# Local-attention layers: the feed-forward's inner rows as one plain float32 tensor, and its second product with unsplit float32 weights

## What is computed

```python
def _layer(x, wqkv, qs, ksc, wo, lg, lb, w1, b1, w2, b2):
    h = shift_token(x)
    ...                                  # q, k, v, norm, rotary, local attention
    x = x + o @ wo
    h = shift_token(x)
    ...                                  # layer norm with lg, lb
    h = h @ w1 + b1                      # 256 -> 2 * 682
    a, g = jnp.split(h, 2, axis=-1)
    h = a * jax.nn.gelu(g, approximate=False)
    x = x + h @ w2 + b2                  # 682 -> 256
    return x
```

## Time and profile before

| | before |
|---|---|
| median of 3 runs | 2409.9 us (2406.12 to 2416.5) |
| profiled execution | 2408.27 us |
| its span in the trace | 2406.0 us |
| PE busy | 2172.1 us, 90% |
| ACT busy | 1452.6 us, 60% |
| DVE busy | 1414.2 us, 59% |
| POOL busy | 1062.7 us, 44% |

### The profile page before, as it was taken

One profiled execution on the slowest core, in us unless ns is written; L12 is line 12 of the kernel. 1 busy time (PEld: TensorE's weight loads), 2 busy tenths in 40 slices (PEclk: granted clock), 3 DMA queues, 4 the chain that ended last, 5 costly groups with the idle time before them and its releaser, 6 DMA issues. The chain is left out here.

```text
span 2406.0 us, 48672 instructions
## 1 busy us (share of the span) xinstructions
PE 2172.1 (90%) x15280; PEld 1787.3 (74%) x15280; DVE 1414.2 (59%) x4204; ACT 1452.6 (60%) x4009; POOL 1062.7 (44%) x1364
## 2 busy tenths in 40 slices
PE   4999999999999977998998999996889999999999
PEld 4777777777767755877877877885678788788778
DVE  3433334244343426866776777675667668677767
ACT  3656666476666645665665566564756755755764
POOL 1333333233333316563464365363636535644644
PEclk9999999899999987999999999998899999999999
DMA  3000100001010012011011001103110110110110
GB/s 105 23 21 20 40 14 29 21 23 36 4 41 13 29 55 83 10 38 39 15 36 37 27 23 42 40 6 99 45 47 14 44 47 14 44 47 16 44 45 23
DMA packets 99051, 84.36 MB, mean 35 GB/s; under 512 B 19601, under 2 KB 93645, under 8 KB 98765
## 3 DMA queue, kind: packets, MB, share of 16 engines
q1 hardware_dynamic: 98764, 80.81, 11.1%
HBM read 55.08 MB, written 17.31 MB: 30 GB/s over the span
## 5 line engine op out<-in xcount | busy, mean ns | idle before, releaser
L403 POOL TENSOR_SCALAR a_prob<-a_prob,a_row_inv,a_gate 128x192 f32<-128x192 f32 x512 | 258.0, 519 | 546.0 <-DVE a_row_inv L692 546.0
L1115 POOL TENSOR_SCALAR f_prob<-f_prob,f_row_inv 128x256 f32<-128x256 f32 x512 | 250.4, 508 | 373.3 <-DVE f_row_inv L1435 373.0
L1154 PE MATMUL f_bank<-f_wqkv,f_actT 128*128 128x512 f32 x1296 | 335.9, 408 | 18.6 <-DVE f_wqkv L1408 15.3
L1154 PEld LDWEIGHTS f_bank<-f_wqkv,f_actT 128*128 128x128 f32 x1296 | 240.5, 193 | 77.9 <-DVE f_wqkv L1408 16.1
L1269 PE MATMUL f_bank<-f_hT,f_w 128*114 128x256 f32 (+1 forms) x2304 | 294.1, 281 | 0.0
L1269 PEld LDWEIGHTS f_bank<-f_hT,f_w 128*114 128x114 f32 (+1 forms) x2304 | 280.3, 176 | 1.5
L1346 ACT ACTIVATE f_prob<-f_scores,f_neg_max 128x256 f32<-128x256 f32 x512 | 237.1, 489 | 61.2 <-DVE f_neg_max L1427 61.2
L594 ACT ACTIVATE a_prob<-a_scores,a_neg_max 128x192 f32<-128x192 f32 x512 | 209.0, 431 | 56.9 <-DVE a_neg_max L684 55.9
L1094 POOL TENSOR_TENSOR f_qk_tok<-f_qk_tok,f_tables 128x512 f32<-128x512 f32 x144 | 185.4, 1308 | 128.1 <-DVE f_sin_part L1391 128.1
L1088 POOL TENSOR_TENSOR f_norm<-f_norm,f_minus_half 128x16 f32<-128x16 f32 x72 | 224.2, 3115 | 14.3 <-DVE f_norm L1383 13.3
L422 PE MATMUL a_bank<-a_xT,a_wqkv 128*128 128x512 f32 x816 | 224.3, 426 | 0.0
(11 more groups left out here) (126 smaller groups left out, 4411.1 us busy)
## 6 DMA issues: line engine op xcount, KB each, us to landing
f_tables<-in_tables SPq DMA_DIRECT2D x18, 512.0 KB, 3.9
a_x_tok<-in_x SPq DMA_DIRECT2D x9, 512.0 KB, 4.4
normed<-a_x_tok SPq DMA_DIRECT2D x9, 512.0 KB, 3.3
f_x_tok<-normed SPq DMA_DIRECT2D x18, 256.0 KB, 4.4
f_x_tok<-hidden SPq DMA_DIRECT2D x18, 256.0 KB, 4.5
a_y_tok<-in_x SPq DMA_DIRECT2D x8, 512.0 KB, 4.7
attended<-a_y_tok SPq DMA_DIRECT2D x8, 512.0 KB, 3.0
f_x<-normed SPq DMA_DIRECT2D x8, 512.0 KB, 4.2
```

The costliest lines, as they stand in the source:

```text
L403: last = nc.gpsimd.tensor_scalar(part, part, row_inv[:, a % 2, head, t:t + 1], gate[:, half, tile + t, h:h + 1], ALU.mult, ALU.mult)
L1115: last = nc.gpsimd.tensor_scalar(part, part, row_inv[:, a % 2, head, t:t + 1], 1.0, ALU.mult, ALU.mult)
L1154: last = nc.tensor.matmul(out, lhs(c, a), rhs(c, b), start=(i == 0), stop=(i == len(order) - 1))
```

## The change

`u` becomes one plain float32 tile, and `w2` one plain float32 tile without parts.

- DVE's product of value and gate (L1486 before) writes `u` itself, and its signal `emptied` now also tells PE that the rows are there. ACT's rounding copy (L1363) and DVE's remainder (L1489) are gone, with the semaphores `u_hi` and `u_ready`. Gelu of a step waits for `emptied` of the step two before it, where it waited for `u_ready`.
- `down` is one plain float32 matmul for each token tile in place of three float32r ones.
- `w2` comes by two transfers straight into its tile, issued by SP behind the last staged piece; PE waits for them in front of the loop, and so does GpSimd, through the raised count. The splits 9 to 11 are gone from the list.

```diff
-        w2 = sb("w2", [P, 2, FH, D], F32R)
+        w2 = sb("w2", [P, FH, D])
...
-        u = sb("u", [P, 2 * TILES, 2, PART], F32R)
+        u = sb("u", [P, 2 * TILES, PART])
...
-                  ("transpose_qk", t0 + 1), ("rope_sum", t0 + 3), ("split", 8), ("transpose_qk", t0 + 2), ("split", 9),
-                  ("transpose_qk", t0 + 3), ("split", 10), ("split", 11)]
+                  ("transpose_qk", t0 + 1), ("rope_sum", t0 + 3), ("split", 8), ("transpose_qk", t0 + 2), 
+                  ("transpose_qk", t0 + 3)]
...
-        for j0, j1, m in ((0, 4, HT), (4, FH - 1, HT), (FH - 1, FH, HL)):
-            r0 = j0 * HT
-            pieces.append((w2_in[r0:r0 + (j1 - j0) * m, :].rearrange("(j p) n -> p j n", p=m), w2[0:m, HI, j0:j1, :], w2[0:m, LO, j0:j1, :]))
...
-        CONSTS, SCALES = 8, 6
+        CONSTS, SCALES = 10, 6
...
             for i in range(4, len(pieces)):
                 stage_piece(i)
+            r1 = (FH - 1) * HT
+            sp.dma_start(w2[0:HT, 0:FH - 1, :], w2_in[0:r1, :].rearrange("(j p) n -> p j n", p=HT)).then_inc(consts_loaded, 16)
+            sp.dma_start(w2[0:HL, FH - 1, :], w2_in[r1:HID, :]).then_inc(consts_loaded, 16)
...
             pe.wait_ge(zeroed, 1)
+            pe.wait_ge(consts_loaded, 16 * CONSTS)
...
                     elif kind == "down":
                         j, m = hidden_of(a)
-                        pe.wait_ge(u_ready.sem, u_ready.past(it, ("up", a)))
+                        pe.wait_ge(emptied.sem, emptied.past(it, ("up", a)))
...
                         for t in (0, 1):
-                            for i, (up, wp) in enumerate(PASSES):
-                                mm = nc.tensor.matmul(y_banks[a // FH % PARTS][:, t, :], u[0:m, a % (2 * TILES), up, t * P:(t + 1) * P],
-                                                      w2[0:m, wp, j, :], start=(j == 0 and t == 0 and i == 0),
-                                                      stop=(j == FH - 1 and t == 1 and i == 2), skip_group_check=True)
+                            mm = nc.tensor.matmul(y_banks[a // FH % PARTS][:, t, :], u[0:m, a % (2 * TILES), t * P:(t + 1) * P],
+                                                  w2[0:m, j, :], start=(j == 0 and t == 0), stop=(j == FH - 1 and t == 1),
+                                                  skip_group_check=True)
...
                         if a >= 2:
-                            act.wait_ge(u_ready.sem, u_ready.past(it, ("up", a - 2)))
+                            act.wait_ge(emptied.sem, emptied.past(it, ("up", a - 2)))
                         nc.scalar.activation(gu[0:m, a % 2, :], bank[n % 3][0:m, PART:2 * PART], ACT.Gelu,
                                              bias=b1_cols[0:m, 1, j:j + 1]).then_inc(gelued.sem, 1)
-
-                        act.wait_ge(emptied.sem, emptied.past(it, (kind, a)))
-                        nc.scalar.activation(u[0:m, a % (2 * TILES), HI, :], gu[0:m, a % 2, :], ACT.Copy).then_inc(u_hi.sem, 1)
...
-                        nc.vector.scalar_tensor_tensor(out=gu[0:m, a % 2, :], in0=bank[n % 3][0:m, 0:PART], scalar=b1_cols[0:m, 0, j:j + 1],
+                        nc.vector.scalar_tensor_tensor(out=u[0:m, a % (2 * TILES), :], in0=bank[n % 3][0:m, 0:PART], scalar=b1_cols[0:m, 0, j:j + 1],
                                                        in1=gu[0:m, a % 2, :], op0=ALU.add, op1=ALU.mult).then_inc(emptied.sem, 1)
-                        dve.wait_ge(u_hi.sem, u_hi.past(it, (kind, a)))
-                        nc.vector.tensor_tensor(u[0:m, a % (2 * TILES), LO, :], gu[0:m, a % 2, :],
-                                                u[0:m, a % (2 * TILES), HI, :].bitcast(F32), ALU.subtract).then_inc(u_ready.sem, 1)
```

2 lines of the change are left out of this document (removed).

## The result

| | before | changed |
|---|---|---|
| median, measured together (20 executions each) | 2405.1 us | 2413.2 us |
| ratio | 1 | 1.0036, interval 1.0023 to 1.0049 |
| measured together once more (17 and 12 executions) | 2407.5 us | 2410.4 us |
| ratio | 1 | 1.0013, interval 0.9996 to 1.0030 |
| profiled execution | 2408.27 us | 2413.38 us |

The change costs some 3 to 8 us, 0.1 to 0.4%. The forecast was 2422.

What follows compares the result with a forecast made beforehand. PE's queue was taken to set the feed-forward parts' length; 29.6 - 13.4 - 2.8 = +13.4 us on the profiled 2408.3 gave 2421.7, stated as 2422 us, 0.5% slower, range 2406 to 2450.

Steps and rivals of the forecast that it cites:

- slower by over 0.5%: Outcome class for the whole kernel, above 2421.9 us; given 0.63, against 0.31 for the same and 0.06 for faster.
- Dearer products, +29.6 us: In 192 `down` steps on PE, four plain records of 0.216 us take 0.864 us instead of 0.71.
- bound of 0.234 (weight load): Rival: full-width weight load makes a `down` record step 0.234 us, term +43.4, sum +27, 2437 us; chance 0.13.
- the one below 0.2: Rival: `down` records under 0.199 us make the change win; one column pass gives -62, 2346 us; chance 0.06.
- the rival of +22: Rival: each of seven `down` runs a half loses 0.2 us changing number format, +22, 2444 us; chance 0.13.
- Waits given back, -13.4 us: In feed-forward parts, PE's removed waits give 8 x 0.32 us in layer 0 and 8 x 1.35 in layer 1.
- I give all of that back: Layer 1's feed-forward part, 33.71 - 32.68 = 1.03 us longer than layer 0's, was taken to lose all of that.
- The stretch's uncovered 0.32 us say that there is no more to have: Layer 0's feed-forward part: only PE's 0.32 us bank wait at `transpose_qk` 2 could be gained.
- the rival of +27: Rival: `rope` and `rope_sum` meet GpSimd's long instructions elsewhere, PE's bank waits stay, +27, 2437 us; chance 0.10.
- Start of the layers, -2.8 us: Without the `w2` splits, PE starts the first scores 1.4 us earlier, twice.
- The attention parts, counted at nothing: The 16 attention parts got no term in the sum; only the clock was allowed 8 us either way.
- The attention parts change their mean length: Sign: the forecast is wrong if the attention parts change their mean length.

Runs made afterwards that it cites:

- bias_later: Kernel before with copy and remainder as a separate, later step, and GpSimd's `x1_bias` waiting until `ln_apply` is through: 2383.2 us, ratio 0.9910.
- work_kept: Changed kernel with ACT's copy and DVE's remainder put back, the remainder going to a tile nobody reads: 2424.6 us, ratio 1.0075.
- longer_float32r: Kernel before with the last of the three `down` passes made twice, eight float32r records instead of six: 2439.5 us, ratio 1.0146.
- again: The changed kernel measured once more, with no further edit, against the kernel before: 2410.4 us, ratio 1.0013.
- changed_bias_later: Changed kernel with GpSimd's `x1_bias` waiting until `ln_apply` is through: 2412.7 us, ratio 1.0035.
- after_moved_code: Changed kernel with semaphore increments nobody waits for at the start of PE, ACT, DVE and SP, so later code lies elsewhere: about 2418 us, ratio 1.0049.
- half_down_2: Changed kernel with the second token tile's `down` matmul only for the first of six pieces: 2348.2 us, ratio 0.9765.

## Why the prediction was near, and where it failed

The verdict was right by its own bounds (2422 forecast, 2413 and 2410 measured, both in the range from 2406), but its most likely class, slower by over 0.5%, was not the outcome, and the sum was 13 us for what is 3 to 8. One term was off by some 11 us. That the time stayed in the range does not speak for this term: the range was made for the clock and for waits that stay, not for more waits to give back, and it had room for the error by luck.

- **Dearer products, +29.6 us: right.** The record steps at 0.216 us, and (33.84 - 32.01) x 16 = 29 us where no wait is left on either side. The bound of 0.234 (weight load) and the one below 0.2 are both refuted.
- **No price for switching: right**, the rival of +22 is refuted by 0.67 + 0.19 = 0.86 us. The runs of `down` cost 1.83 us a half's part in all, which is 12 x 0.153 with seven runs and so with up to 14 changes of kind in it. The 0.2 us around a scores step are then not the price of the number format alone; that they belong to its half-array shape is what is left, and no run tests it. The Trainium skill (TensorEngine Tiling (Array Packing), Key Properties) lays the drain to a change of tiling mode, and the trace agrees: none is seen between `up` and `down`, which both take more than 64 rows and columns of the array.
- **Waits given back, -13.4 us: this step failed.** It should have been about -24. "I give all of that back" took one stretch of each layer, both of them first halves, as 32.68 and 33.71 us, and used it 8 times a layer. With the product's 1.83 us taken off, the change gives back 0.68 and 1.69 us in first halves (0.32 and 1.35 forecast), 9.5 us in all where the forecast had 6.7. Second halves, up to the first exp, take 38.11 us before and 38.10 now, so each gives back 1.84 us, 14.7 us in all where the forecast had 6.7. The error lies in the second halves above all: they held a wait of PE for `ln_apply` ahead of `transpose_h` 1 (0.5 us each by the profile), which is in neither of the stretches that I had read. With this term the sum is 29.3 - 24.2 - 2 = +3 us, and +3 and +8 were measured.
- **"The stretch's uncovered 0.32 us say that there is no more to have": wrong.** bias_later's same part takes 32.01 us against 32.70, so 0.7 us could be had. Matmul records with modelled ends probably cover short waits.
- **Who gives it back.** Not only the freed engines: work_kept puts their share at about 14 us. The other 10 come from longer `down` steps that run inside waits: work_kept has all of the price, 29 us less 2 at the starts, and is only 17 us above the kernel before. longer_float32r shows the same (13 of 45 us with nothing taken off ACT or DVE). The forecast had no such term.
- **"GpSimd draws out any DVE instruction that meets it", in the rival of +27: wrong.** The products of value and gate meet a GpSimd instruction of over 2 us 8 times in the kernel before and last 472 ns at most there; the remainders meet one 16 times and last up to 1640 ns.
- **Start of the layers, -2.8 us: right at its place**, the wait fell by 1.3 us in layer 0. From the first projection to the first scores, layer 1 got 1.4 us shorter (43.01 to 41.62) and layer 0 only 0.1 (42.76 to 42.62), so 1.5 to 2.8 us. Over all profiles with and without the change the starts differ by 0.9 and 1.0 us in the mean, about 2 us together.
- **The attention parts, counted at nothing: nearly right, but they look longer.** "The attention parts change their mean length" was a sign of being wrong. The five profiles with plain products and whole `down` steps have a mean of 53.46 us, the eight with float32r 52.99. Over 16 parts that is 8 us. Some 5 of them are the way from the scores to the exp at the six turns, which moved over the cut and is counted in the waits above. The other 3 or so the forecast had at nothing.
- **What stays open.** The late transfer of the edge row may be a part of what is left. With four late halves in layer 1 (changed) that layer's attention parts are 1.2 us longer in the mean than layer 0's, with three (again) 0.7, with one over 2 us (changed_bias_later, work_kept) 0.4 and 0.1, and with four in layer 0 (after_moved_code) they are 1.2 us shorter; in the kernel before, without any, they are 0.5 us shorter. Against it, half_down_2 has four late halves in layer 1 too, and there the layers are equal. The clock moves single profiles by more: in the changed kernel's profile the granted clock was at 1.2 GHz for 96 us of the attention parts and in that of `again` for 66 us, and the same program's attention parts were 14 us shorter there in all (53.79 and 52.93 us each).

## What to carry to other kernels

Before a wait is priced from one stretch, all the places where the changed step stands must be cut into stretches: the two halves of a loop body and the loop's turn can differ by more than the effect, as 32.7 and 35.0 us do here. When work on the bounding engine gets longer and shorter on its helpers, run or imagine both alone: the longer work fills waits by itself, so price and gain are not additive (29 us of price less 14 us of gain would be 15, and 5 are left). A stretch should end where an engine on the chain does its next work, not just where PE starts something: a wait that shrinks in front of a cut can come back behind it, as the 4.2 us at the loop's turn did. And when an instruction on DVE is dearer than its twins, look at what GpSimd does beside it: here one changed wait on GpSimd and a later place for the remainder gave 22 us, with the cheaper product kept.

## What the chip showed that was not expected

- Plain float32 with 256 columns over the whole array steps at 0.216 us a record, two records a matmul: 0.43 us a product, against 0.355 for three float32r passes; four float32r records would be 0.47.
- Between a plain and a float32r matmul nothing is lost, but the first float32r record behind plain ones starts 0.03 us after the last of them and is itself 0.19 us longer: single starts mislead, the sum does not.
- DVE's `ln_apply` instruction with two SBUF inputs lasted up to 2725 ns instead of 485 beside a GpSimd instruction of 2.5 us on float32 tiles, and GpSimd's own took 2.49 us in the mean beside it and 2.38 alone.
- A small transfer of SP reached DVE 2.4 to 2.7 us behind its issue instead of 1.6 to 1.8 in four halves of layer 1 (three of them again in the repetition, 2.3 to 2.5 us), and in other halves when the code was moved. In the changed kernel its issue on SP took 0.94 to 1.56 us instead of 0.58; in other versions it landed late behind an issue of 0.58.
- At the loop's turn ACT's first exp came 4.2 us behind the last `down`, whether PE started the scores 1.7 us behind it (before) or 1.0 us (changed).
